# Two fused attention and expert layers: the product with the values issued in halves of 256 columns, one half at the start of each step

## The chip, the cores and the metric

The kernel runs on one core of a Trainium2 chip, in one launch. The metric is the device time of that launch in microseconds, the median over runs. TensorE multiplies, VectorE and ScalarE read its results out of PSUM, GpSimd prepares operands, SyncE issues DMAs; each engine works through its own queue in order, and they meet at semaphores.

## The reference, cut to what matters

The reference is two transformer layers on x of 4 x 1024 x 256. Each is attention, then a feed-forward part with experts, each with layer norms and a residual. The change touches only the attentions, which both have 16 heads of 16 columns:

```
# attention 0
attn = softmax(einsum('bhnd,bhmd->bhnm', q, k) / sqrt(256))
out  = einsum('bhnm,bhmd->bhnd', attn, v)
# attention 1: position slopes, causal
scores = q @ k.T / sqrt(16) + slopes * (pos_k - pos_q)
attn = softmax(where(pos_k <= pos_q, scores, -inf))
out  = einsum('bhqk,bhkd->bhqd', attn, v)
```

## The kernel before, in words

The function `attention` is built twice, as attention 0 (not causal) and attention 1 (causal). The work of one of them is 32 *slots*; in a slot two heads of one batch row are done, for all 1024 queries. While a slot computes exponentials and value products of its own pair of heads (`e`), it also computes the row maxima and the transposes for the next pair (`m`), and the transposes and first maxima of the one after it (`a`). The pairs alternate between two halves of the buffers. A hardware loop holds two slots.

A slot has NS steps: 16 in attention 0, (2 chunks of 512 queries) x (8 key tiles of 128), and 12 in attention 1, where chunk 0 has only 4 key tiles. At step n:

- TensorE computes the transposed scores of a key tile against 512 queries for both heads (`qk`, line 255; in attention 1 the diagonal tiles get a mask added, line 234, and only the columns right of `first_col` are computed). ScalarE turns them into exponentials in `pr` (`exp`, line 339). `pr` has 4 places.
- TensorE computes one tile of scores in the other orientation (`scores`, line 243), and VectorE takes its row maxima (`rowmax`, lines 379 and 385). These maxima enter the next pair's queries, so that the exponentials need no subtraction. Step 7 of attention 1 has none.
- Both kinds of tile share three buffers S of two PSUM banks each, in a fixed ring. In attention 0 `qk` of step n takes the buffer that the maxima of step n-2 have read, and `scores` of step n the one that the exponential of step n-1 has read.
- Every odd step, TensorE multiplies the exponentials of two steps with the values (`pv`, line 271): four matmuls of 32 output rows side by side, for 2 heads x 2 key tiles, up to 512 columns, accumulating in OP, one PSUM bank. They are f32, and each shows as two records. At the end of a chunk ScalarE copies OP to `ot` (`evac_o`, line 342), TensorE transposes it (`finish`, line 279), and VectorE adds, divides by the sum and stores (`add`, `scale`). Before a new chunk's first product TensorE waits for that copy (`o_read`, line 274).
- In steps 0, 10 (6 in attention 1), 8 (4) and NS-2 TensorE transposes new queries or keys into the bank TP (`fill`, line 228), and ScalarE copies them (`evac`, line 336), in steps NS-5 and NS-1 ahead of the exponential of that step. `finish` shares TP, in steps 4 and KEYS0+1 (12 or 8).
- At step TURN = NS-4 (12 or 8) all row maxima of the next pair are there; VectorE reduces them, TensorE transposes them (`turn_max`, line 285, "the turn" below), VectorE copies them out (line 408) and SyncE's DMA places them in the queries. The turn takes a place in the ring too; in attention 1 its place is the one that the exponential of step 7 has read.

All orders are written out by hand in `slot`, once for each engine. The group of two steps that `pv` handles is g; at step n it is g = (n-2)//2, and at n = 1 the last group of the slot before.

Of the kernel before, what the change touches and what calls it, by code (L numbers as in the profile page):

```python
# [36 lines left out]
def attention(nc, tag, qkv, ao, causal, exp_scale, ident_d, aug_d=None, masks_d=None, ahead=None):  # L37

    with Mem(nc,tag) as m:
# [5 lines left out]
        vn=sb("vn",[128,2,TILES,2,32])  # L45
        qT=sb("qT",[128,2,SEQ],F32R)
        kT=sb("kT",[128,2,SEQ],F32R)
        pr=sb("pr",[128,4,2,512])
# [24 lines left out]
        def first_col(c,kt):  # L73
            return 0 if (not causal or kt<2) else max(0,kt*128-c*512)
# [8 lines left out]
        CHUNK0=(4 if causal else TILES)//2  # L83
        GROUPS_PV=NS//2
        last_groups=(CHUNK0-1,GROUPS_PV-1)
        O_FULL0=2*CHUNK0+1
        KEYS0=NS-EARLY-1
        QUERIES0=2*CHUNK0
        TURN=NS-EARLY
# [14 lines left out]
        with nc.Block() as block:  # L104
# [108 lines left out]
            def _(pe):  # L213
# [32 lines left out]
                def qk(s,n):  # L246
                    c,kt=steps[n]
                    b=ring["e",n]
                    if n==0: pe.wait_ge(m_placed,32).then_inc(m_placed,-32)
                    pe.wait_ge(s_free[b],1).then_inc(s_free[b],-1)  # L250
                    f=first_col(c,kt)
                    diag=causal and kt*128>=c*512
                    for h in range(2):
                        r=slice(64*h,64*h+64)
                        mm=pe.matmul(S[:,b,h,f:512],kT[r,s,kt*128:kt*128+128],qT[r,s,c*512+f:c*512+512],start=True,stop=not diag)  # L255
                    if diag:
                        e=kt*128-c*512+128
                        w=e-f
                        for j in range(2):
                            for h in range(2): mm=masked(S[:,b,h,f:e],h,slice(512-w,512),j)  # L260
                    mm.then_inc(exp_full,1)
                def exp_read(n):

                    freed=s_free[ring["e",n]]
                    pe.wait_ge(freed,1).then_inc(freed,-1); pe.sem_inc(freed,1)  # L265
                def pv(s,g):
                    if g==0: pe.wait_ge(v_ready[s],1).then_inc(v_ready[s],-1)
                    for h in range(2):
                        for x in range(2):
                            n=2*g+x; c,kt=steps[n]; f=first_col(c,kt); j=2*h+x  # L270
                            mm=pe.matmul(OP[32*j:32*j+32,f:512],vn[:,s,kt,h,:],pr[:,n%4,h,f:512],start=kt<2,stop=g in last_groups,skip_group_check=True)  # L271
                    if g in last_groups: mm.then_inc(o_full,1)
                def o_read(free_v=None):
                    pe.wait_ge(ot_ready,1).then_inc(ot_ready,-1)
                    if free_v is not None: pe.sem_inc(v_free[free_v],1)
# [10 lines left out]
                def slot(e,prev,m,after):  # L286


                    a=None if not after else 1-m
                    for n in range(NS):  # L290
                        if e is not None: qk(e,n)
                        x,ahead=max_at(n)
                        if m is not None and n==0: t_bank_read()
                        if a is not None and n==NS-EARLY: t_bank_read()
                        s=a if ahead else m
                        unit=x is not None and s is not None
                        if unit: scores(s,x)
                        if m is not None and n==TURN: turn_max()
                        if m is not None and n==0: fill(m,0,1)
                        if m is not None and n==2: t_bank_read(); pe.sem_inc(nat_free[m],1)  # L300
                        if a is not None and n==QUERIES0: fill(a,1,0)
                        if a is not None and n==KEYS0-1: fill(a,0,0)
                        if a is not None and n==NS-2: fill(a,1,1)
                        g=(n-2)//2 if n>1 else GROUPS_PV-1
                        who=prev if n<2 else e
                        if who is not None:
                            if n%2==0 and not unit: exp_read(2*g+1)
                            if n%2==1:
                                if g in (0,CHUNK0): o_ready(g,e,prev)
                                pv(who,g)  # L310
                        if prev is not None and n==4: finish()
                        if e is not None and n==KEYS0+1: finish()
                def o_ready(g,e,prev):
                    if g==0 and prev is not None: o_read(free_v=prev)
                    if g==CHUNK0: o_read()
                fill(0,1,0); fill(0,0,0)
                t_bank_read()
                for x in range(EARLY): scores(0,x)
# [3 lines left out]
                with pe.Fori(1,BATCH*GROUPS-1):  # L322
                    slot(0,1,1,True); slot(1,0,0,True)
                slot(0,1,1,False); slot(1,0,None,False)
                exp_read(NS-1)
                pv(1,GROUPS_PV-1)
                o_read()
                finish()

            @block.scalar  # L330
            def _(act):
                nc.scalar.preload_act_table(ACT.Exp)
                def evac(s,f,half):
                    act.wait_ge(half_full,1).then_inc(half_full,-1)  # L334
                    cols=slice(half*512,half*512+512)
                    nc.scalar.activation((kT,qT)[f][:,s,cols],TP[:],ACT.Copy).then_inc(half_copied,1)  # L336
                def exp(n):
                    c,kt=steps[n]; f=first_col(c,kt)
                    nc.scalar.activation(pr[:,n%4,:,f:512],S[:,ring["e",n],:,f:512],ACT.Exp,scale=exp_scale).then_inc(s_free[ring["e",n]],1)  # L339
                def evac_o():  # L340
                    act.wait_ge(o_full,1).then_inc(o_full,-1)
                    nc.scalar.activation(ot[:],OP[:],ACT.Copy).then_inc(ot_ready,1)
                def slot(e,prev,m,after):
                    a=None if not after else 1-m
                    for n in range(NS):
                        if e is not None: act.wait_ge(exp_full,1).then_inc(exp_full,-1)  # L346
                        if a is not None and n==KEYS0: evac(a,0,0)
                        if a is not None and n==NS-1: evac(a,1,1)
                        if e is not None: exp(n)
                        if m is not None and n==1: evac(m,0,1)  # L350
                        if prev is not None and n==1: evac_o()
                        if e is not None and n==O_FULL0: evac_o()
                        if a is not None and n==QUERIES0: evac(a,1,0)
                evac(0,1,0); evac(0,0,0); evac(0,1,1)
                slot(None,None,0,True)
                slot(0,None,1,True); slot(1,0,0,True)
                with act.Fori(1,BATCH*GROUPS-1):
                    slot(0,1,1,True); slot(1,0,0,True)
                slot(0,1,1,False); slot(1,0,None,False)
                evac_o()  # L360
# [1331 lines left out]
```

## Time and profile before

| | |
|---|---|
| median of 3 runs | 3406.16 us (3405.43 to 3414.36) |
| the profiled execution's own time | 3403.33 us |
| its span, from first to last instruction | 3401.6 us |
| TensorE busy | 2729.3 us, 80% |
| VectorE busy | 1966.6 us, 58% |
| ScalarE busy | 1625.9 us, 48% |
| value products (line 271) | 3584 records, 564 ns mean |
| probability scores (line 255) | 1792 records, 472 ns mean |
| score tiles for the maxima (line 243) | 1792 records, 430 ns mean |
| exponentials (line 339) | 896, 941 ns mean |

A busy time is the union of an engine's records; records of matmuls overlap, so their mean is not their cost, and the distance from one start to the next tells more. An engine's idle time matters only where another engine's next work hangs on it.

### The profile page before, as it was taken

How to read it: one execution, taken by the hardware profiler on the slowest of the kernel's cores; microseconds unless marked ns; L12 is line 12 of the kernel's file. 1: busy time of each engine (PE TensorE's matmuls, PEld its weight loads, DVE VectorE, ACT ScalarE, POOL GpSimd, SP SyncE). 2: the span in 40 equal slices, each digit the busy share in tenths (PEclk: the TensorE clock that was granted, in tenths of full speed). 3: DMA queues.
4: the chain of work that ended last, by engine and by line, in shares of the span. 5: the costliest groups of instructions: out<-in, count | busy, mean ns of one | idle time of the engine just before them, and what ended most of it. 6: DMA issues, size and time to landing. Idle time of an engine off the chain costs nothing. (4 is left out here: it accounts for less than half of the span.)

```text
span 3401.6 us, 63393 instructions
## 1 busy us (share of the span) xinstructions
PE 2729.3 (80%) x16332; PEld 1619.0 (48%) x16333; DVE 1966.6 (58%) x4600; ACT 1625.9 (48%) x2553; POOL 959.6 (28%) x1653
## 2 busy tenths in 40 slices
PE   8699999999977449995399959688888887718887
PEld 5333333333324438874388724344444444415554
DVE  3488888888845353335533354576667754556641
ACT  3277777777754433333333334366666663302212
POOL 1411111111126115541155444322222213403333
PEclk9699999999995569995599979799999996759999
DMA  6501010010013102214022166111111104322331
GB/s 168 168 20 24 14 25 19 19 25 13 19 40 113 56 16 69 68 58 149 14 69 68 59 174 183 44 26 25 31 26 30 25 10 121 119 92 70 99 100 61
DMA packets 365685, 215.08 MB, mean 63 GB/s; under 512 B 284782, under 2 KB 345842, under 8 KB 364791
## 3 DMA queue, kind: packets, MB, share of 16 engines
q1 hardware_dynamic: 231224, 106.71, 11.8%
q10 hardware_dynamic: 116416, 54.53, 5.5%
q0 software_dynamic: 17920, 52.46, 4.9%
q8 instruction: 43, 0.70, 0.1%
q14 instruction: 82, 0.67, 0.1%
HBM read 129.20 MB, written 85.98 MB: 63 GB/s over the span
## 5 line engine op out<-in xcount | busy, mean ns | idle before, releaser
L339 ACT ACTIVATE att_pr<-att_S 128x1024 f32<-128x1024 f32 (+1 forms) x896 | 836.1, 941 | 427.5 <-ACTq L346 424.4
L379 DVE TENSOR_REDUCE att_mparts<-att_S 128x2 f32<-128x1024 f32 x640 | 777.1, 1225 | 169.1 <-DVEq L375 165.2
L255 PE MATMUL att_S<-att_qT,att_kT 64*128 64x512 f32 (+3 forms) x1792 | 430.0, 472 | 46.4 <-PEq L250 42.1
L271 PE MATMUL att_OP<-att_pr,att_vn 128*32 128x512 f32 (+3 forms) x3584 | 451.1, 564 | 1.0 <-PEq L265 0.7
L243 PE MATMUL att_S<-att_kT,att_qT 64*128 64x512 f32 (+3 forms) x1792 | 391.0, 430 | 74.1 <-PEq L237 62.7
L255 PEld LDWEIGHTS att_S<-att_qT,att_kT 64*128 64x128 f32 x1792 | 175.0, 184 | 471.9 <-issue 460.7
L179 POOL COPY att_vn<-att_raw 128x256 f32<-128x256 f32 x64 | 25.4, 396 | 1148.6 <-POOLq L178 1148.6
L243 PEld LDWEIGHTS att_S<-att_kT,att_qT 64*128 64x128 f32 x1792 | 188.0, 190 | 173.0 <-issue 167.1
L385 DVE CUSTOM_DVE_ANT_0 att_unused<-att_S,att_mask 128x128 f32<-128x128 f32 (+3 forms) x512 | 228.3, 488 | 69.9 <-DVEq L375 69.9
L1067 POOL DMA_INDIRECT experts_xs<-scaled,ffn_source x144 | 140.2, 974 | 353.2 <-SPq L1060 163.5
L1164 DVE COPY experts_y<-experts_Y 128x256 f32<-128x256 f32 x144 | 61.2, 425 | 223.3 <-DVEq L1163 223.3
L1138 ACT ACTIVATE experts_hh<-experts_TH 128x512 fp32r<-128x512 f32 x144 | 86.2, 598 | 204.2 <-ACTq L1137 202.7
L1073 POOL DMA_INDIRECT mixed<-experts_y,ffn_target x144 | 146.2, 1016 | 92.5 <-issue 43.1
L1161 DVE TENSOR_TENSOR experts_hl<-experts_TH,experts_hh 128x512 fp32r<-128x512 f32 x144 | 99.6, 692 | 111.8 <-DVEq L1159 111.0
L1141 ACT ACTIVATE experts_h<-experts_H 128x512 f32<-128x512 f32 x144 | 86.2, 599 | 127.5 <-ACTq L1140 127.5
L1406 PE MATMUL ffn_Y<-ffn_w,ffn_hT 128*128 128x256 f32 x512 | 128.5, 402 | 8.9 <-PEq L1405 8.9
L1401 PE MATMUL ffn_H<-ffn_xT,ffn_w 128*128 128x512 f32 x256 | 121.1, 630 | 13.4 <-PEq L1399 9.1
L479 POOL TENSOR_TENSOR post_s<-post_s,post_half 128x2 f32<-128x2 f32 x128 | 97.1, 758 | 115.3 <-POOLq L651 109.1
L675 PE MATMUL post_Y<-post_w,post_aT 128*128 128x256 f32 x256 | 107.2, 563 | 27.8 <-PEq L673 27.8
L271 PEld LDWEIGHTS att_OP<-att_pr,att_vn 128*32 128x32 f32 x3584 | 72.0, 108 | 109.7 <-issue 105.3
L336 ACT ACTIVATE att_qT<-att_TP 128x512 fp32r<-128x512 f32 x128 | 76.1, 594 | 90.5 <-ACTq L334 90.5
L1406 PEld LDWEIGHTS ffn_Y<-ffn_w,ffn_hT 128*128 128x128 f32 x512 | 97.1, 198 | 33.7 <-issue 20.8
(291 smaller groups left out, 4913.0 us busy)
## 6 DMA issues: line engine op xcount, KB each, us to landing
qkv<-qkv_y ACTq DMA_DIRECT2D x64, 384.0 KB, 3.4
att_raw<-qkv SPq DMA_DIRECT2D x96, 256.0 KB, 3.3
rows<-post_rows ACTq DMA_DIRECT2D x32, 384.0 KB, 2.7
ffn_w<-in_w ACTq DMA_DIRECT2D x12, 1024.0 KB
ao<-att_aon SPq DMA_DIRECT2D x32, 256.0 KB, 2.8
post_at<-ao SPq DMA_DIRECT2D x64, 128.0 KB, 3.1
scaled<-rms_zs SPq DMA_DIRECT2D x64, 128.0 KB, 1.7
rms_rows<-mixed SPq DMA_DIRECT2D x32, 256.0 KB, 3.6
```

The source lines that it names most:

```text
L243: mm=pe.matmul(S[:,b,h,at:at+n],qT[r,s,qt*128:qt*128+128],kT[r,s,half*512:half*512+n],start=True,stop=True)
L255: mm=pe.matmul(S[:,b,h,f:512],kT[r,s,kt*128:kt*128+128],qT[r,s,c*512+f:c*512+512],start=True,stop=not diag)
L271: mm=pe.matmul(OP[32*j:32*j+32,f:512],vn[:,s,kt,h,:],pr[:,n%4,h,f:512],start=kt<2,stop=g in last_groups,skip_group_check=True)
L339: nc.scalar.activation(pr[:,n%4,:,f:512],S[:,ring["e",n],:,f:512],ACT.Exp,scale=exp_scale).then_inc(s_free[ring["e",n]],1)
L379: nc.vector.tensor_reduce(mparts[:,s,:,2*qt+half],S[:,b,:,0:width(qt,half)],AX.X,ALU.max).then_inc(end,1)
L385: nc.vector.tensor_tensor_reduce(unused[:,2*i+h,0:n],S[:,b,h,at:at+n],mask[:,512-n:512],1.0,-3.0e38,ALU.add,ALU.max,mparts[:,s,h,2*qt+half ...
L675: mm=pe.matmul(Y[:,u%4,0:DIM],aT[:,u%2,128*k:128*k+128],w[:,k,:],start=k==0,stop=k==KC-1 and not last)
L1067: nc.gpsimd.indirect_dma_start(out=xs[:,t%R,:],out_offset=None,in_=zs_d,in_offset=bass.IndirectOffsetOnAxis(ap=source[:,t:t+1],axis=0)).th ...
L1073: nc.gpsimd.indirect_dma_start(out=y2_d,out_offset=bass.IndirectOffsetOnAxis(ap=target[:,t:t+1],axis=0),in_=y[:,t%RY,:],in_offset=None, bo ...
L1161: V.tensor_tensor(hl[:,u%2],TH[:,u%2,:],hh[:,u%2].bitcast(F32),ALU.subtract).then_inc(hT_ready,1)
L1401: mm=pe.matmul(H[:,c%2,:],w1[:,e%2,k,128*c:128*c+128],xT[:,k,:],start=k==0,stop=k==KC-1)
L1406: if c<FC: pe.matmul(Y[:,t%2,0:DIM],hT[:,c,128*t:128*t+128],w2[:,e%2,c,:],start=c==0,stop=False)
```

## The change

`pv` now takes a piece p instead of a group: group p//2, and of its columns the left 256 (p even) or the right 256 (p odd); columns left of `first_col` are skipped as before, so that in attention 1 the left half of two groups is empty. Piece n-3 is issued at the beginning of step n, ahead of `qk`, in every step; before, a whole group was issued at the end of each odd step, behind `scores`. The wait for the copy of OP (`o_ready`) goes ahead of the pieces 0 and 2*CHUNK0, that is ahead of `qk` of step 3 and of step 11 (7 in attention 1). Only the first half of a bank's first product carries the start flag. ScalarE's `evac_o` moves from the end of step 1 to the beginning of step 2, and from the end of step 9 (5) to the beginning of step 10 (6).

```diff
--- before.py
+++ after.py
@@ -83,7 +83,9 @@
         CHUNK0=(4 if causal else TILES)//2
         GROUPS_PV=NS//2
         last_groups=(CHUNK0-1,GROUPS_PV-1)
-        O_FULL0=2*CHUNK0+1
+        last_pieces=(2*CHUNK0-1,NS-1)
+        LAG=3
+        O_FULL0=2*CHUNK0-1+LAG
         KEYS0=NS-EARLY-1
         QUERIES0=2*CHUNK0
         TURN=NS-EARLY
@@ -263,13 +265,14 @@
 
                     freed=s_free[ring["e",n]]
                     pe.wait_ge(freed,1).then_inc(freed,-1); pe.sem_inc(freed,1)
-                def pv(s,g):
-                    if g==0: pe.wait_ge(v_ready[s],1).then_inc(v_ready[s],-1)
+                def pv(s,p):
+                    g,part=divmod(p,2)
+                    if p==0: pe.wait_ge(v_ready[s],1).then_inc(v_ready[s],-1)
                     for h in range(2):
                         for x in range(2):
-                            n=2*g+x; c,kt=steps[n]; f=first_col(c,kt); j=2*h+x
-                            mm=pe.matmul(OP[32*j:32*j+32,f:512],vn[:,s,kt,h,:],pr[:,n%4,h,f:512],start=kt<2,stop=g in last_groups,skip_group_check=True)
-                    if g in last_groups: mm.then_inc(o_full,1)
+                            n=2*g+x; c,kt=steps[n]; f=max(first_col(c,kt),256*part); j=2*h+x
+                            if f<256*part+256: mm=pe.matmul(OP[32*j:32*j+32,f:256*part+256],vn[:,s,kt,h,:],pr[:,n%4,h,f:256*part+256],start=kt<2 and part==0,stop=g in last_groups,skip_group_check=True)
+                    if p in last_pieces: mm.then_inc(o_full,1)
                 def o_read(free_v=None):
                     pe.wait_ge(ot_ready,1).then_inc(ot_ready,-1)
                     if free_v is not None: pe.sem_inc(v_free[free_v],1)
@@ -288,6 +291,13 @@
 
                     a=None if not after else 1-m
                     for n in range(NS):
+                        g=(n-2)//2 if n>1 else GROUPS_PV-1
+                        who=prev if n<2 else e
+                        p=n-LAG
+                        of=e if p>=0 else prev
+                        if of is not None:
+                            if p in (0,2*CHUNK0): o_ready(p,prev)
+                            pv(of,p%NS)
                         if e is not None: qk(e,n)
                         x,ahead=max_at(n)
                         if m is not None and n==0: t_bank_read()
@@ -301,18 +311,12 @@
                         if a is not None and n==QUERIES0: fill(a,1,0)
                         if a is not None and n==KEYS0-1: fill(a,0,0)
                         if a is not None and n==NS-2: fill(a,1,1)
-                        g=(n-2)//2 if n>1 else GROUPS_PV-1
-                        who=prev if n<2 else e
-                        if who is not None:
-                            if n%2==0 and not unit: exp_read(2*g+1)
-                            if n%2==1:
-                                if g in (0,CHUNK0): o_ready(g,e,prev)
-                                pv(who,g)
+                        if who is not None and n%2==0 and not unit: exp_read(2*g+1)
                         if prev is not None and n==4: finish()
                         if e is not None and n==KEYS0+1: finish()
-                def o_ready(g,e,prev):
-                    if g==0 and prev is not None: o_read(free_v=prev)
-                    if g==CHUNK0: o_read()
+                def o_ready(p,prev):
+                    if p==0 and prev is not None: o_read(free_v=prev)
+                    if p==2*CHUNK0: o_read()
                 fill(0,1,0); fill(0,0,0)
                 t_bank_read()
                 for x in range(EARLY): scores(0,x)
@@ -322,8 +326,9 @@
                 with pe.Fori(1,BATCH*GROUPS-1):
                     slot(0,1,1,True); slot(1,0,0,True)
                 slot(0,1,1,False); slot(1,0,None,False)
+                pv(1,NS-3)
                 exp_read(NS-1)
-                pv(1,GROUPS_PV-1)
+                pv(1,NS-2); pv(1,NS-1)
                 o_read()
                 finish()
 
@@ -343,13 +348,13 @@
                 def slot(e,prev,m,after):
                     a=None if not after else 1-m
                     for n in range(NS):
+                        if prev is not None and n==LAG-1: evac_o()
+                        if e is not None and n==O_FULL0: evac_o()
                         if e is not None: act.wait_ge(exp_full,1).then_inc(exp_full,-1)
                         if a is not None and n==KEYS0: evac(a,0,0)
                         if a is not None and n==NS-1: evac(a,1,1)
                         if e is not None: exp(n)
                         if m is not None and n==1: evac(m,0,1)
-                        if prev is not None and n==1: evac_o()
-                        if e is not None and n==O_FULL0: evac_o()
                         if a is not None and n==QUERIES0: evac(a,1,0)
                 evac(0,1,0); evac(0,0,0); evac(0,1,1)
                 slot(None,None,0,True)
```

## Rows read from the trace of the kernel before

**Rows 1.** The page, busy time of each engine.
```profile
PE 2729.3 (80%) x16332; PEld 1619.0 (48%) x16333; DVE 1966.6 (58%) x4600; ACT 1625.9 (48%) x2553; POOL 959.6 (28%) x1653
```

**Rows 2.** Timeline of TensorE, attention 0: start, length (us), what.
```profile
413.69 0.27 PE L285 MATMUL att_S<-att_ident,att_m 128*16 128x128 f32 x1 [0.47 <-PEq L284]
...
414.32 0.51 PE L255 MATMUL att_S<-att_qT,att_kT 64*128 64x512 f32 x2
...
415.18 1.07 PE L271 MATMUL att_OP<-att_pr,att_vn 128*32 128x512 f32 x8
416.17 0.50 PE L255 MATMUL att_S<-att_qT,att_kT 64*128 64x512 f32 x2
416.51 0.40 PE L243 MATMUL att_S<-att_kT,att_qT 64*128 64x512 f32 x2
...
417.42 0.50 PE L255 MATMUL att_S<-att_qT,att_kT 64*128 64x512 f32 x2
...
419.79 0.50 PE L243 MATMUL att_S<-att_kT,att_qT 64*128 64x512 f32 x2
420.22 0.53 PE L228 MATMUL att_TP<-att_identr,att_kn 128*128 128x128 f32 x4
420.68 0.51 PE L255 MATMUL att_S<-att_qT,att_kT 64*128 64x512 f32 x2
...
423.27 0.49 PE L255 MATMUL att_S<-att_qT,att_kT 64*128 64x512 f32 x2
...
425.96 0.50 PE L255 MATMUL att_S<-att_qT,att_kT 64*128 64x512 f32 x2
...
429.19 0.50 PE L255 MATMUL att_S<-att_qT,att_kT 64*128 64x512 f32 x2
...
432.42 0.51 PE L255 MATMUL att_S<-att_qT,att_kT 64*128 64x512 f32 x2
...
437.54 0.50 PE L243 MATMUL att_S<-att_kT,att_qT 64*128 64x512 f32 x2 [0.26 <-PEq L237]
...
440.15 0.27 PE L285 MATMUL att_S<-att_ident,att_m 128*16 128x128 f32 x1 [0.44 <-PEq L284]
```

**Rows 3.** Timeline of ScalarE in the same slot of attention 0.
```profile
421.31 1.03 ACT L339 ACTIVATE att_pr<-att_S 128x1024 f32<-128x1024 f32 x1 [0.25 <-ACTq L346]
422.24 0.59 ACT L336 ACTIVATE att_kT<-att_TP 128x512 fp32r<-128x512 f32 x1
422.86 0.60 ACT L342 ACTIVATE att_ot<-att_OP 128x512 f32<-128x512 f32 x1
423.35 1.94 ACT L339 ACTIVATE att_pr<-att_S 128x1024 f32<-128x1024 f32 x2
```

**Rows 4.** Timeline of TensorE in a slot of attention 1.
```profile
2419.52 0.63 PE L271 MATMUL att_OP<-att_pr,att_vn 128*32 128x256 f32 x8
2420.08 0.50 PE L255 MATMUL att_S<-att_qT,att_kT 64*128 64x512 f32 x2
...
2421.61 0.50 PE L255 MATMUL att_S<-att_qT,att_kT 64*128 64x512 f32 x2
...
2423.97 0.27 PE L285 MATMUL att_S<-att_ident,att_m 128*16 128x128 f32 x1 [0.15 <-PEq L284]
...
2429.74 0.51 PE L255 MATMUL att_S<-att_qT,att_kT 64*128 64x512 f32 x2
...
2434.26 0.33 PE L255 MATMUL att_S<-att_qT,att_kT 64*128 64x128 f32 x2 [0.28 <-PEq L250]
...
2436.39 0.50 PE L255 MATMUL att_S<-att_qT,att_kT 64*128 64x512 f32 x2
```

**Rows 5.** Timeline of ScalarE in the same slot of attention 1.
```profile
2422.81 2.06 ACT L339 ACTIVATE att_pr<-att_S 128x1024 f32<-128x1024 f32 x2
...
2433.70 0.60 ACT L342 ACTIVATE att_ot<-att_OP 128x512 f32<-128x512 f32 x1
```

**Rows 6.** Timeline of VectorE in the same slot of attention 1.
```profile
2429.36 0.08 DVE L385 DVE_READ_ACCUMULATOR2_ANT att_mparts<- 128x1 f32 x1
```

## The prediction

> **What bounds the kernel now.** I read the page first. TensorE is busy 80% of the span and the next engine, VectorE, 58% [rows 1], so an edit that adds work to TensorE or makes it wait has little cover. The page cannot say which wait ends last inside a step, so I went to the timelines of TensorE and of ScalarE, one slot of each attention, and read distances from the start of one instruction to the start of the next.
>
> In attention 0 a slot, from one turn of the maxima to the next, takes 440.15 - 413.69 = 26.46 us for 16 steps [rows 2]. Below, qk(n), sc(n) and exp(n) are step n's probability scores, score tile for the maxima, and exponential. The steps go in pairs, and most pairs take 3.23 us: qk(4) at 425.96, qk(6) at 429.19, qk(8) at 432.42 [rows 2]. A pair with four transposes in it takes no more than one without. So it isn't the sum of TensorE's work that sets the pair. The ring does: sc(n) uses the S buffer that exp(n-1) has read. From qk(even) it is 0.63 us to exp (420.68 to 421.31, [rows 2, 3]), 1.03 for exp, 0.14 until sc(odd) may start (exp 7 ends at 2422.81 + 1.03, the turn that waits for it starts at 2423.97, [rows 4, 5]), so 1.80; then 0.43 of sc and 0.99 of a whole value product (415.18 to 416.17) before the next qk(even) [rows 2]. 1.80 + 0.43 + 0.99 = 3.22. The 3.23 are explained, and the whole value product lies on that ring.
>
> Attention 1 has 12 steps. Its turn, at 2423.97, waits for exp(7) [rows 4, 5]; qk(0), at 2429.74, comes 0.30 us after VectorE has read the masked maximum at 2429.36 + 0.08 [rows 4, 6]; qk(4) follows the turn by 12.42 us.
>
> **The change part by part.** (a) *ScalarE's order.* Moving the copy of OP from the end of step 1 (and 9, or 5) to the beginning of step 2 (and 10, or 6) changes no position in its queue: exp, the transposed copy, copy of OP, next exp, as before. The "step later" costs and gives nothing; nor is a DMA moved. (b) *TensorE's order.* The second half of a value product stands at the beginning of the even step, which is where the old product ended. So what really moves is the first half: it goes ahead of qk(odd) and sc(odd). (c) The wait for the copy of OP and the release of v go with it, ahead of qk(3), and of qk(11) or qk(7). No new race-guarding wait arises: exp of both steps is already waited for by the score tile of the step before.
>
> *Price of a half.* In attention 1 a group with no more than 256 columns takes 2420.08 - 2419.52 = 0.56 us to the next start [rows 4], against 0.99 for 512 [rows 2]. So 0.43 goes by columns and 0.13 is fixed. Two halves cost 1.12: +0.13 per split product, 8 a slot in attention 0 and 4 in attention 1 (two of its six are single halves already). The Trainium skill, TensorEngine Tiling (Array Packing), section Instruction Overhead, puts about 60 cycles on each matmul; with 8 more records per product that would be an estimated 0.20 us a product instead, if none overlapped. The sum goes by the rows.
>
> *Gain.* On the even ring only a half is left: 1.80 + 0.43 + 0.56 = 2.79 us a pair instead of 3.23, a gain of 0.44.
>
> *What takes its place.* qk(odd) now comes one half later than sc(even), and exp(odd) gates the next sc(even). The odd ring: 1.80 (qk(odd) to sc(even)), 0.38 to what follows (0.33 in the stretch directly behind a value product, as 416.17 to 416.51; 0.43 after a wait, 419.79 to 420.22; I take the middle), 0.46 for four transposes (420.22 to 420.68), 0.56 for the half: 3.2 us with transposes, 2.74 without [rows 2]. Transposes stand in the even steps 0, 4, 8, 10, 12, 14. So only the pair of step 6 runs at 2.79, and pair 2 might.
>
> Now a slot of attention 0, in stretches, new against old [rows 2, 3]:
> 1. Turn to qk(1): old 420.68 - 413.69 = 6.99. New: qk(13) at 0.63 + 0.56 = 1.19; sc(14) at 1.19 + 1.80 = 2.99; transposes 3.37, half 3.84, qk(15) 4.40 (old 417.42 - 413.69 = 3.73). ScalarE puts a transposed copy ahead of exp(15), so sc(0) follows qk(15) by 419.79 - 417.42 = 2.37: 6.77. Then 0.43, 0.46 and a half, 0.56: qk(1) at 8.22. **+1.23.**
> 2. qk(1) to qk(4): old 5.28. New: ScalarE does exp(1) at 0.63, kT copy 1.56 (0.93 later), copy of OP 2.05 (0.49 later, as from 422.86 to 423.35 between a copy and the next instruction), done 2.65. TensorE then has two waits and a signal to go through: after the kT copy (422.24 + 0.59 = 422.83) it took 0.44 until qk(3) at 423.27. So the half starts at 3.09, qk(3) 3.65, sc(3) 3.98, second half 4.42, qk(4) 4.98. **-0.30.** If TensorE woke in 0.14, it would be 0.3 less.
> 3. qk(4) to qk(8): old 6.46. New: pair 4 with the transposes of ot: sc 0.48, 0.38, 0.55 (turn and such transposes together took 0.63, 413.69 to 414.32), half 0.56, sc(5) 0.33, 0.43, half 0.56 = 3.29; pair 6 2.79. Sum 6.08. **-0.38.**
> 4. qk(8) to the turn: old 440.15 - 432.42 = 7.73. New: pair 8: 0.48 + 0.38 + 0.47 + 0.56 + 0.33 + 0.43 + 0.56 = 3.21; from qk(10) to sc(11) 0.48 + 0.38 + 0.47 + 0.56 + 0.33 = 2.22; sc(11) to the turn is VectorE's last maximum and its reduction, unchanged 440.15 - 437.54 = 2.61. The old product behind sc(11) lay in that wait for free, so halving it gains nothing. Sum 8.04. **+0.31.**
> Together +0.86 us a slot, x32 slots = **+28 us**. With 0.14 for the wake and 0.33 for every distance in doubt it is about +0.2 a slot; with 0.43 everywhere +1.05.
>
> A slot of attention 1 [rows 4 to 6]: the first half now stands ahead of qk(7), which starts 0.56 after the old 2421.61. ScalarE takes qk(7)'s signal before it copies kT and does exp(7), and the turn waits for exp(7): turn up to +0.56. The turn also waits for the last maximum; because in some slots that ends it, I take +0.43 (bounds 0 and 0.56). From the turn VectorE (copy, add, four masked maxima) carries the delay to qk(0) unchanged. Then step 3: the copy of OP ends at 2433.70 + 0.60 = 2434.30, 0.44 to wake, half 2434.74, qk(3) 2435.30 instead of 2434.26, 0.94 for mask, scores and what follows, half 0.56: qk(4) at 2436.80 instead of 2436.39: +0.41 (0.11 if it wakes in 0.14). Together +0.84, x32 = **+27 us**; bounds +0.1 and +1.0, so 3 to 32 us.
>
> **Sum.** 3403.3 (the profiled execution's own time, 1.7 us of it outside the span) + 28 + 27 = 3458 us; the median of the runs is 3 us higher than that execution, so 3461, rounded to 3460. Outside the attentions nothing is touched. The first and last slots differ by less than a microsecond.
>
> **Rivals.**
> - *The smoothing pays.* If exp(odd) doesn't gate sc(even), pairs with transposes go by TensorE's sum, 3.21 - 0.15 = 3.06 instead of 3.24. That is -0.17 in each of five pairs, -0.44 in pair 6, and stretch 1 loses its +0.7 of lateness: about -1.0 a slot, -32 us, with attention 1 between 0 and +27: 3374 to 3402. It speaks for it that pair 6 surely shortens and TensorE idles up to 1 us in stretches. Against: ScalarE needs 1.80 us after each qk whatever its place. It decides if sc(even) starts 0.33 after qk(even) rather than 0.48. Chance 0.14.
> - *The waits hide it.* The wake is quick and attention 1's turn stays bound by the maxima: +0.2 x 32 + 0.1 x 32 = +10 us, 3416; a little less is no change. Chance 0.13.
> - *Half of it.* Only the turn of attention 1 and stretch 1 lengthen, each by half the amount: about +28 us, 3434. Chance 0.18.
> - *Dearer halves.* If a half costs not 0.56 but 0.60 us, because the group of [rows 4] was cheaper than a half among score tiles, 16 halves a slot of attention 0 and 6 of attention 1 bring 0.04 each more: 22 x 0.04 x 32 = 28 us, 3488. Chance 0.05. By the Trainium skill's overhead, named above, a half would cost some 0.59.
> - The forecast, 3445 to 3475 by its own range: 0.50.
>
> **How the numbers follow.** Time 3460 us. A run tells apart about 0.3%, 10 us. Slower by more: 0.50 + 0.18 + 0.05 + a third of the hidden case = 0.77; within: 0.10, the rest of the hidden case and the rim of the first rival; faster 0.13. The range leaves out most of the first rival and the dearer halves: 3395 to 3475.
>
> **What would show it.** Per product two groups on TensorE, 0.56 apart from what follows. Pair 6 at 2.8 us; pairs 8 and 14 at 3.2 with sc(even) 0.48 after qk(even). Turn to turn 27.3 us in attention 0 and 0.8 us more than now in attention 1. TensorE's wait for the copy of OP ahead of the half in step 3, 0.44 after the copy ends. Idle time ahead of the turn in attention 0 grown from 0.44 to about 0.9. The prediction is wrong if turn to turn shrinks in attention 0, or if attention 1's turn stays 2.36 us behind the old place of qk(7).

## The result, and the profile after

The change makes the kernel slower: 3456.5 us (3451.5 to 3462.2, 4 runs) against 3405.8 us of the kernel before on the same chip, a ratio of 1.0147, 95% interval 1.0121 to 1.0173. The forecast was 3460. The profiled execution's span is 3453.7 us, 52.1 more than before.

The page of the changed kernel, busy time of each engine, answers to [rows 1]:

```profile
PE 2770.4 (80%) x19404; PEld 1674.8 (48%) x19405; DVE 1967.1 (57%) x4600; ACT 1623.8 (47%) x2553; POOL 958.3 (28%) x1653
```

TensorE is busy 41 us longer, and its share is the same. From that alone one could think that the additional instructions are the 52 us; the experiments show that they are not.

The same kind of line for the turn of the maxima gives the length of a slot in each attention: count, shortest/median/longest, then the first and last start. First the kernel before, then the changed one (first line attention 0, second attention 1):

```profile
L285 PE MATMUL att_S<-att_ident,att_m x32: 269/269/372, 148.0 to 970.4; 128*16 128x128 f32 x32
L285 PE MATMUL att_S<-att_ident,att_m x32: 269/270/380, 2161.2 to 2790.5; 128*16 128x128 f32 x32
```

```profile
L288 PE MATMUL att_S<-att_ident,att_m x32: 269/270/373, 148.5 to 1001.8; 128*16 128x128 f32 x32
L288 PE MATMUL att_S<-att_ident,att_m x32: 269/270/372, 2193.1 to 2838.2; 128*16 128x128 f32 x32
```

Over 31 slots attention 0 went from (970.4 - 148.0)/31 = 26.53 to (1001.8 - 148.5)/31 = 27.53 us, attention 1 from 20.30 to 20.81. That is 31 and 16 us. Of the remaining 5 us, 4.4 lie behind the last turn: that stretch took 611.1 us before (3401.6 - 2790.5) and 615.5 after. It begins with the end of attention 1, which is in the changed order too. Windows from the last turn to the end of the last value product, before and after; the columns are length, busy of PE, PEld, DVE, ACT and POOL, mean granted clock as a share of 2.4 GHz, busy share of the DMA engines and their GB/s:

```profile
2790.49:2811.37 20.88, 17.53 (x161) 8.50 (x159) 3.09 (x10) 13.08 (x18) 0.00 (x0) 0.99 0.01 1
2838.17:2864.70 26.53, 22.50 (x207) 11.44 (x207) 3.09 (x10) 12.72 (x18) 0.00 (x0) 0.81 0.01 2
```

So the end of attention 1 is 5.7 us longer, at a lower mean clock, and all that follows is 1.2 us shorter. The end of attention 0 has grown too, from 25.8 to 30.0 us between the same two marks, while the stretch from there to the first turn of attention 1 is 3.7 us shorter. In the other kernels below that stretch took 1160.8 to 1165.5 us (b apart), so its 3.7 us cannot be put down to the change.

The timeline of TensorE in a slot of attention 0, which answers to [rows 2] (L257 is qk, L245 sc, L274 a value product, L230 transposes, L288 the turn):

```profile
423.33 0.27 PE L288 MATMUL att_S<-att_ident,att_m 128*16 128x128 f32 x1
...
427.81 0.50 PE L257 MATMUL att_S<-att_qT,att_kT 64*128 64x512 f32 x2
...
430.19 0.50 PE L245 MATMUL att_S<-att_kT,att_qT 64*128 64x512 f32 x2 [0.43 <-PEq L239]
...
431.65 0.50 PE L257 MATMUL att_S<-att_qT,att_kT 64*128 64x512 f32 x2
...
434.73 0.64 PE L274 MATMUL att_OP<-att_pr,att_vn 128*32 128x256 f32 x8 [0.77 <-PEq L270]
...
436.53 0.49 PE L257 MATMUL att_S<-att_qT,att_kT 64*128 64x512 f32 x2
...
439.92 0.50 PE L257 MATMUL att_S<-att_qT,att_kT 64*128 64x512 f32 x2
...
442.72 0.50 PE L257 MATMUL att_S<-att_qT,att_kT 64*128 64x512 f32 x2
...
448.36 0.40 PE L245 MATMUL att_S<-att_kT,att_qT 64*128 64x512 f32 x2
...
450.39 0.50 PE L245 MATMUL att_S<-att_kT,att_qT 64*128 64x512 f32 x2 [0.65 <-PEq L239]
450.86 0.27 PE L288 MATMUL att_S<-att_ident,att_m 128*16 128x128 f32 x1
```

And ScalarE in the same slot, which answers to [rows 3]:

```profile
433.68 0.60 ACT L347 ACTIVATE att_ot<-att_OP 128x512 f32<-128x512 f32 x1
...
448.74 0.60 ACT L341 ACTIVATE att_kT<-att_TP 128x512 fp32r<-128x512 f32 x1 [0.92 <-ACTq L339]
449.23 1.94 ACT L344 ACTIVATE att_pr<-att_S 128x1024 f32<-128x1024 f32 x2
```

Read it by the forecast's stretches:

| Stretch | before | forecast | measured |
|---|---|---|---|
| turn to qk(1) | 6.99 | 8.22 | 431.65 - 423.33 = 8.32 |
| qk(1) to qk(4) | 5.28 | 4.98 | 436.53 - 431.65 = 4.88 |
| qk(4) to qk(8) | 6.46 | 6.08 | 442.72 - 436.53 = 6.19 |
| of it, qk(6) to qk(8) | 3.23 | 2.79 | 442.72 - 439.92 = 2.80 |
| qk(8) to the turn | 7.73 | 8.04 | 450.86 - 442.72 = 8.14 |
| slot | 26.46 | 27.32 | 27.53 |

The "before" column is one of two kinds of slot that took turns before, of about 26.45 and 26.6 us; the changed kernel's usual slots all take about 27.54.

The pair without transposes does get its 0.43 us. The lateness ahead of qk(1) and ahead of the turn costs more. The odd ring shows in this trace as the forecast had it: sc(8), at 443.29, follows qk(7), at 441.49, by 1.80 us. In step 3 the first half waits 0.77 us; it starts 0.45 us after the copy of OP has ended (433.68 + 0.60 = 434.28, then 434.73). Ahead of the turn stands a wait that the forecast had put one instruction later: sc(12) waits 0.65 us for exp(11), which starts at 449.23 because the copy of kT (448.74) is ahead of it.

Attention 1, TensorE, which answers to [rows 4] (the last line is the next turn):

```profile
2444.74 0.27 PE L288 MATMUL att_S<-att_ident,att_m 128*16 128x128 f32 x1 [0.41 <-PEq L287]
...
2455.03 0.64 PE L274 MATMUL att_OP<-att_pr,att_vn 128*32 128x256 f32 x8 [0.66 <-PEq L270]
...
2456.93 0.50 PE L257 MATMUL att_S<-att_qT,att_kT 64*128 64x512 f32 x2
...
2462.48 0.64 PE L274 MATMUL att_OP<-att_pr,att_vn 128*32 128x256 f32 x8
2463.05 0.51 PE L257 MATMUL att_S<-att_qT,att_kT 64*128 64x512 f32 x2
...
2465.42 0.27 PE L288 MATMUL att_S<-att_ident,att_m 128*16 128x128 f32 x1 [0.44 <-PEq L287]
```

and ScalarE, which answers to [rows 5]:

```profile
2453.97 0.60 ACT L347 ACTIVATE att_ot<-att_OP 128x512 f32<-128x512 f32 x1
...
2463.76 0.60 ACT L341 ACTIVATE att_kT<-att_TP 128x512 fp32r<-128x512 f32 x1 [0.93 <-ACTq L339]
2464.26 1.94 ACT L344 ACTIVATE att_pr<-att_S 128x1024 f32<-128x1024 f32 x2
```

From qk(4) to the turn it is now 2465.42 - 2456.93 = 8.49 us. From the turn to qk(4) it is 12.19, and 12.44 in the slot after it; before it was 12.24 and, in the slot of [rows 4], 12.42. So all of the growth stands between qk(4) and the turn. The turn comes 0.14 us after exp(7), 2464.26 + 1.02, as the forecast said; and exp(7) stands behind the copy of kT, which waits for qk(7).

### The profile page after: what moved, and what is told of

It reads as the page before. It is cut to its first block and busy times, and to the rows that moved or that the text cites. A ratio compares the mean times of both kernels' runs of the same rounds, so it can differ in the third digit from the quotient of the medians.

```text
span 3453.7 us, 69537 instructions
## 1 busy us (share of the span) xinstructions
PE 2770.4 (80%) x19404; PEld 1674.8 (48%) x19405; DVE 1967.1 (57%) x4600; ACT 1623.8 (47%) x2553; POOL 958.3 (28%) x1653
## 5 line engine op out<-in xcount | busy, mean ns | idle before, releaser
L274 PE MATMUL att_OP<-att_pr,att_vn 128*32 128x256 f32 (+1 forms) x6656 | 535.7, 388 | 54.1 <-PEq L270 48.4
L257 PE MATMUL att_S<-att_qT,att_kT 64*128 64x512 f32 (+3 forms) x1792 | 432.0, 477 | 12.7 <-PEq L252 8.1
L245 PE MATMUL att_S<-att_kT,att_qT 64*128 64x512 f32 (+3 forms) x1792 | 392.1, 433 | 60.1 <-PEq L239 46.1
L257 PEld LDWEIGHTS att_S<-att_qT,att_kT 64*128 64x128 f32 x1792 | 170.9, 185 | 368.6 <-issue 367.1
L245 PEld LDWEIGHTS att_S<-att_kT,att_qT 64*128 64x128 f32 x1792 | 187.4, 191 | 154.9 <-issue 143.7
L274 PEld LDWEIGHTS att_OP<-att_pr,att_vn 128*32 128x32 f32 x6656 | 133.8, 108 | 243.3 <-issue 225.9
L680 PE MATMUL post_Y<-post_w,post_aT 128*128 128x256 f32 x256 | 105.9, 557 | 28.2 <-PEq L678 28.1
L398 DVE TENSOR_REDUCE att_osum<-att_TP 128x136 f32<-128x272 f32 x128 | 56.3, 439 | 108.3 <-DVEq L396 108.3
```

Source lines behind the costliest of these rows:

```text
L245: mm=pe.matmul(S[:,b,h,at:at+n],qT[r,s,qt*128:qt*128+128],kT[r,s,half*512:half*512+n],start=True,stop=True)
L274: if f<256*part+256: mm=pe.matmul(OP[32*j:32*j+32,f:256*part+256],vn[:,s,kt,h,:],pr[:,n%4,h,f:256*part+256],start=kt<2 and part==0,stop=g ...
L680: mm=pe.matmul(Y[:,u%4,0:DIM],aT[:,u%2,128*k:128*k+128],w[:,k,:],start=k==0,stop=k==KC-1 and not last)
```

## The experiments

All of them are one edit of the kernel before: a table says for each odd step where its value product stands. "whole" is the kernel before; "late" is two halves at the end of the odd step; "early" is the first half ahead of qk(odd), the second at the end of the step, which with every step is the changed order; "mid" is the first half between qk(odd) and sc(odd); "wearly" is the undivided product ahead of qk(odd).

```diff
+        MODE={...}   # per attention: odd step -> place
-                def pv(s,g):
+                def pv(s,g,part=None):
+                    lo,hi=(0,512) if part is None else (256*part,256*part+256)
...
-f=first_col(c,kt); j=2*h+x
-mm=pe.matmul(OP[32*j:32*j+32,f:512],...,pr[:,n%4,h,f:512],start=kt<2,...)
+f=max(first_col(c,kt),lo); j=2*h+x
+if f<hi: mm=pe.matmul(OP[32*j:32*j+32,f:hi],...,pr[:,n%4,h,f:hi],start=kt<2 and part!=1,...)
...
+                        if mode in ("early","wearly"): first()
                         if e is not None: qk(e,n)
+                        if mode in ("mid","wmid"): first()
...
-                                pv(who,g)
+                        if mode in ("whole","late"): first()
+                        if mode in ("late","early","mid"): pv(who,g,1)
```

`first()` is the wait for the copy of OP, where there is one, and the first half (or the whole). The three groups of runs were each timed against the kernel before on their own chip, whose medians were 3405.9 (a to d), 3407.6 (e to h) and 3409.4 us (i to k).

| Run | median us | ratio, 95% interval | slot of attention 0 | of attention 1 |
|---|---|---|---|---|
| the change | 3456.5 | 1.0147 (1.0121 to 1.0173) | 27.53 | 20.81 |
| a: halves in the old place | 3408.9 | 0.9999 (0.9985 to 1.0012) | 26.62 | 20.30 |
| b: whole, ahead of qk | 3689.5 | 1.0829 (1.0800 to 1.0858) | 31.24 | 23.61 |
| c: first half between qk and sc | 3404.7 | 0.9997 (0.9984 to 1.0010) | 26.29 | 20.40 |
| d: change, 13, 15, 1 late | 3443.4 | 1.0098 (1.0066 to 1.0131) | 27.03 | 20.80 |
| e: change, 3 late | 3441.6 | 1.0105 (1.0090 to 1.0119) | 27.52 | 20.41 |
| f: change, 7 of attention 1 late | 3452.5 | 1.0131 (1.0116 to 1.0145) | 27.52 | 20.66 |
| g: kernel before, only step 7 of attention 0 early | 3390.3 | 0.9952 (0.9940 to 0.9965) | 26.10 | 20.26 |
| h: kernel before, in attention 0 7 early, 3 and 9 mid | 3379.7 | 0.9917 (0.9904 to 0.9929) | 25.61 | 20.36 |
| i: change, 11 late | 3448.2 | 1.0122 (1.0106 to 1.0139) | 27.24 | 20.81 |
| j: change, 15 late | 3452.6 | 1.0126 (1.0109 to 1.0143) | 27.32 | 20.80 |
| k: change, six places late | 3404.1 | 0.9981 (0.9971 to 0.9990) | 26.32 | 20.31 |

Slots are means over 31 distances from turn to turn in one trace each. A group of 256 or 512 columns that stands by itself in TensorE's queue, between score tiles, is called a visit below.

**a. Halves in the old place.** A rival had come up with the result: 8 more groups in a slot of attention 0 and 4 in one of attention 1, at the forecast's 0.13 us, over 32 slots, are 50 us, the whole loss.

```diff
-MODE: every odd step "whole"
+MODE: every odd step "late"
```

> The kernel before with each value product in two halves of 256 columns, both where the whole one was, at the end of the odd step. Theory 'late exponentials' (the loss comes from what the first half delays when it stands ahead of qk of the odd step): only the fixed 0.13 us a split is paid, and only where the product lies on the ring, some 4 to 5 of 8 a slot in attention 0 and 2 of 4 in attention 1: 0.6 x 32 + 0.26 x 32 = +28 us, about 3434. Rival 'fixed cost' (the loss is simply 0.13 us for each of 12 more groups a slot, 0.13 x 12 x 32 = 50 us, wherever they stand): 3456, as with the change.

No difference was measured, 0.9999, and both expectations were too high. TensorE's timeline of this kernel shows why:

```profile
413.16 1.07 PE L273 MATMUL att_OP<-att_pr,att_vn 128*32 128x256 f32 x16
414.16 0.50 PE L256 MATMUL att_S<-att_qT,att_kT 64*128 64x512 f32 x2
```

Sixteen records instead of eight take 1.00 us to the next start, the whole product took 0.99 [rows 2]. Dividing costs nothing here; the 0.13 us is paid for each visit, when TensorE goes from the score tiles to the value products and back. The Trainium skill, TensorEngine Tiling (Array Packing), section Key Properties, says that changing the tiling mode drains TensorE. The trace fits that, with 0.57 us for a half that stands alone and 0.50 for each of two that stand together, but it does not show that the cost is a drain. The overhead of some 60 cycles a matmul, which the section Instruction Overhead of that page of the Trainium skill gives, does not show: 8 more records took 0.01 us.

**b. The whole product early.**

```diff
-MODE: every odd step "whole"
+MODE: every odd step "wearly"
```

> The kernel before with each whole value product (no halves) moved ahead of qk of its odd step, with the wait for the copy of OP. 'Late exponentials': no split is paid, but each odd qk and its exponential come 0.99 us later instead of 0.56, so pairs with transposes take 3.64 us, the stretch from turn to qk(1) grows by 2.5, the slot of attention 0 by about 4.2 us and that of attention 1 by about 1.2: 3406 + 136 + 38 = about 3580. 'Fixed cost': no more instructions than before, so 3406.

3689.5 us: with no instruction more than the kernel before, moving the product ahead of qk costs 284 us, in attention 0 4.7 us a slot. Its TensorE, two pairs of steps of which the first has no transposes:

```profile
416.75 0.50 PE L256 MATMUL att_S<-att_qT,att_kT 64*128 64x512 f32 x2
...
418.55 0.49 PE L244 MATMUL att_S<-att_kT,att_qT 64*128 64x512 f32 x2 [0.83 <-PEq L238]
418.97 1.06 PE L273 MATMUL att_OP<-att_pr,att_vn 128*32 128x512 f32 x8
419.96 0.50 PE L256 MATMUL att_S<-att_qT,att_kT 64*128 64x512 f32 x2
...
421.76 0.50 PE L244 MATMUL att_S<-att_kT,att_qT 64*128 64x512 f32 x2 [0.70 <-PEq L238]
...
422.66 1.06 PE L273 MATMUL att_OP<-att_pr,att_vn 128*32 128x512 f32 x8
423.66 0.50 PE L256 MATMUL att_S<-att_qT,att_kT 64*128 64x512 f32 x2
```

From qk(odd), 416.75 and 419.96, to sc(even), 418.55 and 421.76, it is 1.80 and 1.80 us. This is the odd ring of the forecast as the bound: 1.80 + 0.42 + 0.99 = 3.21, with transposes 1.80 + 0.43 + 0.47 + 1.00 = 3.70 a pair. The rival "fixed cost" had 3406. The size was under-forecast, by 0.5 us a slot in attention 0 and by 2.1 in attention 1. Part of it is the clock, whose mean from the first to the last turn is 0.97 and 0.94 in this kernel, against 0.99 and 0.99 before. The slots of attention 1 at full clock take 22.9 to 23.0 us, so 2.6 us of the 3.3 come with the order and 0.7 with the clock; how the 2.6 come about was not taken apart.

**c. The first half between qk and sc.**

```diff
-MODE: every odd step "whole"
+MODE: every odd step "mid"
```

> Halves, but the first one stands between qk and sc of the odd step, where TensorE waits for the exponential of the even step anyway; the second at the end of the odd step. 'Late exponentials': no odd exponential is late, the even ring keeps only one half: a slot of attention 0 25.6 to 25.8 us instead of 26.5, attention 1 +0.1 us: 3406 - 26 + 3 = about 3383. 'Fixed cost': as many groups as with the change, 3456.

3404.7 us, not distinguishable from before. This kernel makes as many visits as the changed one, and is 52 us faster: the loss is in the place, not in the number. But the expected gain did not come either, a slot is 26.29 instead of 25.6 to 25.8. Its pair of steps 6 and 7:

```profile
426.13 0.50 PE L256 MATMUL att_S<-att_qT,att_kT 64*128 64x512 f32 x2
...
427.16 0.51 PE L256 MATMUL att_S<-att_qT,att_kT 64*128 64x512 f32 x2 [0.29 <-PEq L251]
...
429.16 0.50 PE L256 MATMUL att_S<-att_qT,att_kT 64*128 64x512 f32 x2
```

qk(7) waits 0.29 us; its S buffer is read by VectorE's maximum of step 5, which starts at 425.79, behind the addition of the chunk before, and ends at 427.02 in VectorE's timeline. qk to qk is 3.03 instead of 2.79. The same kind of wait, 0.29 us ahead of qk(3), stands in the stretch before. In this order a late qk(odd) is followed by a half, so that sc(odd) comes late with it.

**d. Steps 13, 15 and 1 late.**

```diff
-MODE attention 0: every odd step "early"
+MODE attention 0: 13, 15, 1 "late", else "early"
```

> The changed order, except that in steps 13, 15 and 1 of attention 0 both halves stand at the end of the step, where the whole product was. 'Late exponentials': the stretch from the turn to qk(1) goes back from 8.32 to about 7.15 us, the one after it loses 0.2, so the slot is 26.6 instead of 27.5 us: 3456 - 30 = about 3426. 'Fixed cost': the number of groups is the same, 3456.

3443.4 us and a usual slot of 26.87 us: these steps carry 0.67 of the 1.0 us. The mean of 27.03 has another thing in it. Two windows, of a usual slot and of the next, columns as in the section on the result:

```profile
175.00:202.00 27.00, 24.68 (x219) 11.21 (x219) 21.17 (x24) 19.10 (x23) 3.99 (x9) 1.00 0.10 21
202.00:230.50 28.50, 26.60 (x220) 11.82 (x220) 21.57 (x25) 19.46 (x23) 3.99 (x9) 0.94 0.09 20
```

In four of its 31 slots the slot takes 28.1 to 28.3 us, and the granted clock, at full (2.4 GHz) in the slot ahead, is 0.94 in the one shown here. The changed kernel's slots of attention 0 have none of this. So some 1.3 x 4 = 5 us of this run's time go with the clock. (e has two such slots, at 29.0 us.)

**e. Step 3 late in both attentions.**

```diff
-MODE: every odd step "early"
+MODE: 3 "late", else "early"
```

> The changed order, except that in step 3 of both attentions the whole first product, in two halves, and the wait for the copy of OP stand at the end of the step, as before. By the prediction's step 'the copy of OP' (0.41 us a slot of attention 1 and, against a quick wake, 0.3 in attention 0): 3456 - 13 to - 20, so about 3440. By the trace of the changed kernel, where turn to qk(4) in attention 1 is no longer than before and in attention 0 the first half fills a wait: attention 0 loses about 0.2 a slot, attention 1 gains about 0.2, 3450 to 3458, no change from 3456.

3441.6 us. The forecast's own step, that the first half waits for the copy of OP, was right, and my later reading of the trace, that undoing it would change nothing, was not: a pair of slots of attention 1 takes 20.40 + 20.59 instead of 20.67 + 20.88, so 0.28 us a slot. In attention 0 it is below 0.1, since there the half fills a wait. Of the 15 us by which the median is lower, the usual slots of attention 1 are some 8, and 4 are its first slot, of which the last section tells.

**f. Step 7 of attention 1 late.**

```diff
-MODE attention 1: every odd step "early"
+MODE attention 1: 7 "late", else "early"
```

> The changed order, except that in step 7 of attention 1 the value product stands at the end of the step in two halves, as before. If the loss of attention 1 comes from qk(7) and with it exp(7) and the turn being 0.56 us late, its slot goes from 20.79 back to about 20.4 us and the run to about 3456 - 13 = 3443. Rival: it comes from the other odd steps or the number of groups, then 3456.

3452.5 us, and 0.15 us a slot (20.40 + 20.86 in a pair). Together with e that is 0.43, and a usual slot of attention 1 has grown by just that, from (20.13 + 20.56)/2 = 20.35 to 20.78. The step is real, but smaller than expected, and undoing it pays in only one of two slots. The traces show why, if both kinds of slot are cut into the same stretches (medians over 13 slots of each kind, first kind / second kind):

| Attention 1 | before | the change | e: 3 late | f: 7 late |
|---|---|---|---|---|
| turn to qk(1) | 7.30 / 7.48 | 6.99 / 7.19 | 6.99 / 7.19 | 7.30 / 7.48 |
| qk(1) to qk(4) | 4.94 / 4.95 | 5.21 / 5.22 | 4.95 / 4.95 | 5.21 / 5.21 |
| qk(4) to qk(7) | 5.53 / 5.53 | 6.10 / 6.10 | 6.10 / 6.10 | 5.53 / 5.53 |
| qk(7) to the turn | 2.36 / 2.61 | 2.37 / 2.37 | 2.37 / 2.37 | 2.37 / 2.61 |

The half ahead of qk(7) makes it 0.57 us late in both kinds. In the second kind the kernel before had the turn held by something else, VectorE's reduction of the maxima, as the forecast said of "some slots"; that hid 0.25 of the 0.57. Before, then after:

```profile
2444.04 0.19 DVE L405 TENSOR_REDUCE att_m<-att_mparts 128x16 f32<-128x32 f32 x1 [0.44 <-DVEq L403]
2444.53 0.27 PE L285 MATMUL att_S<-att_ident,att_m 128*16 128x128 f32 x1
```

```profile
2485.52 0.19 DVE L410 TENSOR_REDUCE att_m<-att_mparts 128x16 f32<-128x32 f32 x1 [0.44 <-DVEq L408]
2486.32 0.27 PE L288 MATMUL att_S<-att_ident,att_m 128*16 128x128 f32 x1 [0.41 <-PEq L287]
```

Before, the turn came 0.30 us after the reduction had ended, now 0.61. And whenever the turn is late, the way from it to qk(1) is 0.3 us shorter, in both kinds; with step 7 undone it is back at its old length. So the net price of step 7 is 0.57 - 0.31 = 0.26 and 0.57 - 0.25 - 0.29 = 0.03 us, and that of step 3, 0.27, is paid in both kinds.

**g. Only step 7 of attention 0.**

```diff
-MODE attention 0: every odd step "whole"
+MODE attention 0: 7 "early", else "whole"
```

> The kernel before with one product of attention 0 alone changed: that of step 7 in halves, the first ahead of qk(7). The pair of steps 6 and 7 is the one pair without transposes, so its odd exponential delays nothing: 2.80 us instead of 3.23, the slot 26.1 instead of 26.5, and 32 slots bring 14 us: 3392, ratio 0.996. Rival (each visit to the value products costs 0.13 on the path, smoothing gives nothing): 3410.

3390.3 us, ratio 0.9952 (0.9940 to 0.9965), as expected. The pair, on TensorE:

```profile
424.87 0.50 PE L256 MATMUL att_S<-att_qT,att_kT 64*128 64x512 f32 x2
...
425.53 0.64 PE L273 MATMUL att_OP<-att_pr,att_vn 128*32 128x256 f32 x8
426.10 0.49 PE L256 MATMUL att_S<-att_qT,att_kT 64*128 64x512 f32 x2
426.67 0.51 PE L244 MATMUL att_S<-att_kT,att_qT 64*128 64x512 f32 x2
...
427.67 0.50 PE L256 MATMUL att_S<-att_qT,att_kT 64*128 64x512 f32 x2
```

2.80 us from qk(6) to qk(8). sc(7) starts 0.57 after qk(7), when exp(6) is done, 1.80 after qk(6).

**h. Three places.**

```diff
-MODE attention 0: every odd step "whole"
+MODE attention 0: 7 "early", 3 and 9 "mid", else "whole"
```

> The kernel before with three products of attention 0 changed: step 7 as in the kernel with one, steps 3 and 9 in halves with the first between qk and sc, where TensorE waits 0.74 and 0.17 us for an exponential. Expected 0.43 + about 0.4 + 0.1 us less a slot, 25.55 instead of 26.5: 3406 - 30 = 3376, ratio 0.991. Rival: VectorE's row maxima, which have about 0.3 us of idle time a step, take up part of it as in the kernel with the half behind every qk: 3385 to 3392.

3379.7 us, ratio 0.9917 (0.9904 to 0.9929): faster than the kernel before by 0.8% and than the changed one by 2.2%. The slot of attention 0 is (941.9 - 147.9)/31 = 25.61 by its turns:

```profile
L287 PE MATMUL att_S<-att_ident,att_m x32: 269/270/372, 147.9 to 941.9; 128*16 128x128 f32 x32
```

**i. Step 11 late.**

```diff
-MODE attention 0: every odd step "early"
+MODE attention 0: 11 "late", else "early"
```

> The changed order, except that in step 11 of attention 0 the product stands at the end of the step in two halves. If the last stretch (from qk(8) to the turn, 8.14 us against 7.73 before) is long because sc(11) comes late ahead of the row maximum that the turn waits for, it goes back to about 7.75: the slot 27.14 instead of 27.54, 3456 - 13 = 3443. Rival: the stretch is long by the number of groups, then no change, 3456.

3448.2 us, 27.24 us a slot: 0.29 of the expected 0.40. sc(11) follows qk(8) by 5.22 us instead of 5.62, and the turn is earlier with it.

**j. Step 15 late.**

```diff
-MODE attention 0: every odd step "early"
+MODE attention 0: 15 "late", else "early"
```

> The changed order, except that in step 15 of attention 0 alone the product stands at the end of the step in two halves. The queries' transposed copy stands ahead of exp(15) on ScalarE, and sc(0) of the next slot follows qk(15) by 2.37 us. If that is what the lateness of step 15 costs, the slot loses 0.5 to 0.6 of its 1.0 us: 26.97, 3456 - 18 = 3438. Rival: steps 13 and 1 carry it and step 15 nothing, 3456.

3452.6 us, 27.32 us a slot: 0.21 instead of 0.5 to 0.6.

```profile
425.79 0.50 PE L256 MATMUL att_S<-att_qT,att_kT 64*128 64x512 f32 x2 [0.27 <-PEq L251]
...
428.16 0.50 PE L244 MATMUL att_S<-att_kT,att_qT 64*128 64x512 f32 x2 [0.19 <-PEq L238]
...
429.61 0.50 PE L256 MATMUL att_S<-att_qT,att_kT 64*128 64x512 f32 x2
```

sc(0) follows qk(15) by 2.37 us, as expected. But qk(15) now waits 0.27 for VectorE and starts at 4.24 after the turn at 421.55, instead of the 3.9 that I had for it; the first halves of steps 13 and 1 stay where they were. The three steps of d carry their 0.67 together.

**k. Six places late.**

```diff
-MODE: every odd step "early"
+MODE attention 0: 11, 13, 15, 1 "late", else "early"
+MODE attention 1: 3, 7 "late", else "early"
```

> The changed order with all places undone that the trace holds to be the costly ones: steps 1, 11, 13 and 15 of attention 0, steps 3 and 7 of attention 1; first halves stay ahead of qk in steps 3, 5, 7 and 9 of attention 0 and 1, 5, 9 and 11 of attention 1. If these places carry the whole loss, the gain of the pair of step 6 comes out: slots of about 26.2 and 20.35 us, 3406 - 8, so 3390 to 3406. Rival, a cost in every group: at least half of the loss stays, 3425 or more.

3404.1 us, ratio 0.9981 (0.9971 to 0.9990). All of the loss is gone, though four products a slot of attention 0 and those of steps 1, 5, 9 and 11 of attention 1 still have a first half ahead of qk. The places carry the loss. The slot of 26.3 us keeps 0.2 of the 0.43 that the pair of step 6 brings; by subtraction the other changes of order still cost 0.2. The pair of step 4, 3.39 us instead of 3.23 and 3.30, is one place where that shows.

## Why the prediction was right, and where a term was off

- **Odd ring** (first half ahead of qk(odd), exp(odd) gates sc(even)): shown. Experiment b has it as the bound at 1.80 us, c and a exclude the number of instructions, and k shows that the loss goes with the order in six places.
- **ScalarE's order unchanged, "a step later" in name only**: the copy of OP stands behind the copy of kT and ahead of the next exponential in the timeline after, as in [rows 3].
- **Gain of one half in the pair of step 6**: 2.80 us, forecast 2.79; alone, in g, it is worth 0.5% of the kernel's time.
- **Turn to qk(1)**: +1.33 in the slot shown, +1.18 in the other kind, forecast +1.23. d gives 0.67 of a slot back when its three steps are undone. The split over the single steps was less clean than the forecast's chain, which had each delay pass on in full: j alone gives 0.21.
- **Copy of OP and the wake**: 0.45 us from the end of the copy to the half, forecast 0.44. Its price in attention 1 was 0.28 us a slot by e, forecast 0.41.
- **Step 11 and the turn**: +0.41 in the stretch, forecast +0.31; i gives 0.29 back. The instruction that waits is sc(12), held by exp(11) behind the copy of kT, where the forecast had the turn's own wait.
- **Attention 1**: usual slots grew by 0.43 us, some 13 of the 16 us, against a forecast of 0.84 or 27 us, so the term was nearly twice what was measured. The turn itself was right: from qk(4) it comes 0.57 and 0.32 us later in the two kinds of slot, 0.45 on the average, forecast 0.43. Step 3 was put at 0.41 and is 0.27. What the forecast had wrong is the step behind the turn, that the delay is carried on unchanged: from the turn to qk(1) each slot takes back 0.3 us. So step 7 costs 0.15 net, and 0.45 + 0.27 - 0.30 = 0.42 us explains the growth of 0.43.
- **"The first and last slots differ by less than a microsecond"**: wrong. From the last turn to the last value product it is 4.2 us more in attention 0, at full clock in both kernels, and 5.7 more in attention 1, there in part with the clock (0.99 and 0.81): with step 3 late, in e, the same stretch is 1.5 us longer than before at full clock. The first slot of attention 1 grew by 4.6.
- **Price of a half**: 0.57, forecast 0.56, but the 0.13 in it belongs to the visit and not to the number of matmuls. Where the two halves stand together it is paid once. For the changed order, in which every half stands alone, the sum came out the same.

The total, 3456.5 against 3460, is nearer than its parts, and that is luck: from first to last turn, attention 0 was forecast 3 us too low and attention 1 some 11 too high, and about 5 us outside these were in no sum. Of the 16 us of attention 1, 4.6 are its first slot, which no term foresaw, and its last distance is 1.0 us shorter than before. Two slips of 0.01 in the forecast's arithmetic (416.51 - 416.17 is 0.34, and 3.24 - 3.06 is 0.18) change nothing.

What stays open: how attention 1 comes to lose 2.6 us a slot at full clock in b, where the 0.3 us behind a late turn come from, and how the end of attention 0 comes to lose 4.2 us where a usual one loses 1.0.

## What to carry to other kernels

Before work is moved ahead of an instruction on the busiest engine, ask for each instruction behind it whose start it delays, and what hangs on that one on the other engines: the same half of 0.56 us gained 0.43 ahead of one qk and cost 0.15 to 0.3 ahead of others. A uniform rule over an unrolled schedule mixes the two kinds: applied everywhere it made the kernel 1.5% slower, and with the places chosen one by one the kernel became 0.8% faster. And a fixed cost read from a lone group should be tested by putting two of them side by side, before it is multiplied by a count.

## What the runs showed of the hardware that was not expected

A part of a value product's cost is paid for each visit and not for each matmul: 8 records of 512 columns 0.99 us, 16 records of 256 columns 1.00, but 0.57 for 8 records of 256 columns alone, so 1.14 for two visits.

The clock takes part. The first slot of attention 1 begins at half clock in both kernels. Windows of the kernel before and of the changed one, from about the first turn to the next, columns as above:

```profile
2161.00:2179.50 18.50, 15.54 (x106) 9.02 (x107) 12.47 (x38) 9.54 (x14) 4.00 (x10) 0.77 0.07 16
```

```profile
2193.00:2216.00 23.00, 20.46 (x122) 11.27 (x122) 12.88 (x41) 10.00 (x14) 4.00 (x10) 0.54 0.06 12
```

Over the 18 us ahead of it both stand at 0.50, the lower level of 1.2 GHz, with TensorE busy 10.3 us. In the slot itself the kernel before comes to a mean of 0.77 and takes 18.2 us from turn to turn; the changed one comes to 0.54, so it is at 1.2 GHz nearly throughout, with TensorE busy 20.5 of 23 us, and takes 22.8 us. These 4.6 us happen once and are part of the 16 us of attention 1. The slot goes with the order of the products, but not with it alone. It took 22.8 us in all four kernels whose attention 1 has the changed order (the change, d, i and j), 22.1 in f and 18.8 in e. With attention 1 as before it took 18.2 in the kernel before and 18.1 in g, but 20.0 in h, at a mean clock of 0.65. It was 18.2 in a and k and 18.5 in c. What decides it stays open.
